# A language-model block on one core: a new order for the first four batches, and the last batch's expert results gathered from blocks kept in order

## The reference

```python
h = tok_ref(x, quantum_params, post_w, post_b)            # gather angles, circuit, 6 -> 192
h = h + attn_ref(layernorm(h), W_qkv, b_qkv)              # one head of 192, softmax(q k / sqrt(192)) v
gate = layernorm(h) @ Wg                                  # 8 scores; the top 2, softmax over them
h = h + sum_k share_k * (gelu(layernorm(h) @ W1[e_k] + b1[e_k]) @ W2[e_k] + b2[e_k])
```

## Time and profile before

| what | us |
|---|---|
| median of 3 runs (lowest, highest) | 286.31 (284.52, 288.8) |
| the profiled execution | 288.43 |
| its span, first to last instruction | 286.7 |
| PE busy (share of the span) | 209.2 (73%) |
| DVE busy | 171.9 (60%) |
| ACT busy | 120.8 (42%) |
| POOL busy | 200.2 (70%) |

### The profile page before, as it was taken

One profiled execution on the slowest core, in us unless ns is written; L12 is line 12 of the kernel. 1 busy time (PEld: TensorE's weight loads), 2 busy tenths in 40 slices (PEclk: granted clock), 3 DMA queues, 4 the chain that ended last, 5 costly groups with the idle time before them and its releaser, 6 DMA issues.

```text
span 286.7 us, 5700 instructions
## 1 busy us (share of the span) xinstructions
PE 209.2 (73%) x1559; PEld 149.3 (52%) x1559; DVE 171.9 (60%) x651; ACT 120.8 (42%) x293; POOL 200.2 (70%) x273
## 2 busy tenths in 40 slices
PE   0760599278877699698688899999999999992000
PEld 0550454123444244445446797787899998982000
DVE  5754899978797995856755586233477003532223
ACT  1001213454454332656446364655566676661000
POOL 5777787707992657477676777777777777777750
PEclk9999999755596755779656799999999999999555
DMA  7911001189900000000012211133333229985763
GB/s 152 297 24 14 4 3 13 13 322 363 322 8 1 9 13 14 9 14 14 13 39 52 56 37 27 43 99 90 102 89 92 76 75 328 351 247 165 237 223 117
DMA packets 26074, 29.85 MB, mean 104 GB/s; under 512 B 15162, under 2 KB 19889, under 8 KB 25851
## 3 DMA queue, kind: packets, MB, share of 16 engines
q1 hardware_dynamic: 19564, 21.54, 24.7%
q0 software_dynamic: 6480, 7.94, 9.2%
HBM read 14.13 MB, written 16.02 MB: 105 GB/s over the span
## 4 chain that ended last, share of the span: by engine, by line
PE 49%; DVE 23%; POOL 9%; issue 7%; ACT 5%; DMA 4%; DVEq 1%; POOLq 0%; ACTq 0%; SPq 0%
PE bank_b L2132 22%; PE bank_b L1886 6%; PE bank_a L2120 5%; POOL circuit L562 5%; PE bank_a L1893 4%; POOL shares_out L767 4%; PE bank_c L1905 3%; DVE nmax L1194 3%; ACT prob L1602 2%; DMA shares_out<-circuit,up 2%; PE bank_d L1844 2%; ACT keys_t L1580 1%; DVE circuit L881 1%; DVE form_s L1165 1%; DVE form_p L1161 1%
## 5 line engine op out<-in xcount | busy, mean ns | idle before, releaser
L767 POOL DMA_INDIRECT shares_out<-circuit,up x71 | 73.7, 1038 | 21.6 <-issue 16.8
L733 POOL DMA_INDIRECT routed<-rows,slot x64 | 62.5, 976 | 31.0 <-issue 16.5
L2132 PE MATMUL bank_b<-wide,up 128*128 x426 | 79.1, 336 | 1.7 <-issue 1.4
L2132 PEld LDWEIGHTS bank_b<-wide,up 128*128 128x128 f32 x426 | 68.9, 192 | 7.2 <-issue 5.5
L1765 ACT ACTIVATE circuit<-bank_b,up 128x192 f32<-128x192 f32 x71 | 29.9, 422 | 29.5 <-PE bank_b L2132 28.0
L562 POOL DMA_INDIRECT circuit<-angles,ids x32 | 31.7, 991 | 11.0 <-issue 9.1
L1753 ACT ACTIVATE up<-bank_a 128x384 f32<-128x384 f32 x71 | 34.3, 486 | 9.0 <-PE bank_a L2120 8.4
L1893 PE MATMUL bank_a<-keys_t,wt 32*128 32x512 f32 x64 | 27.4, 944 | 3.3 <-ACT keys_t L1580 1.9
L1886 PE MATMUL bank_b<-queries_t,keys_t 32*128 32x512 f32 x64 | 25.1, 866 | 4.9 <-ACT keys_t L1580 2.5
L1194 DVE TENSOR_REDUCE nmax<-bank_a 128x2 f32<-128x1024 f32 x16 | 19.5, 1219 | 9.3 <-PE bank_a L1893 9.3
L1602 ACT ACTIVATE prob<-bank_b 128x1024 f32<-128x1024 f32 x16 | 16.4, 1023 | 18.8 <-PE bank_b L1886 18.8
(11 more groups left out here) (438 smaller groups left out, 379.1 us busy)
## 6 DMA issues: line engine op xcount, KB each, us to landing
routed<-pad_rows SPq DMA_DIRECT2D x8, 528.0 KB, 5.3
out<-hres SPq DMA_DIRECT2D x7, 384.0 KB, 5.7
wide<-down_w SPq DMA_DIRECT2D x1, 2304.0 KB, 11.9
prob<-shares_out SPq DMA_DIRECT2D x3, 768.0 KB
up<-up_w SPq DMA_DIRECT2D x1, 1536.0 KB
angle_stages<-shares_out SPq DMA_DIRECT2D x2, 768.0 KB, 6.8
form_p<-shares_out SPq DMA_DIRECT2D x2, 768.0 KB, 6.8
up<-routed SPq DMA_DIRECT2D x71, 16.0 KB, 1.8
```

The costliest lines, as they stand in the source:

```text
L733: pool.indirect_dma_start(out=routed, out_offset=bass.IndirectOffsetOnAxis(slot[:, b, k, j:j + 1], 0), in_=rows[:, b, k, j, :], in_offset=None
L767: pool.indirect_dma_start(out=shares_out, out_offset=bass.IndirectOffsetOnAxis(xb[:, m, DEST:DEST + 1].bitcast(I32), 0), in_=y[:, m % RESU ...
L2132: mm = pe.matmul(bank_b[:, m % 2, 0:D], hid[:, m % STEP, c * P:(c + 1) * P], wide_flat[:, bass.ds(first + c * D, D)], start=(c == 0), stop ...
```

## The change

Four parts. (1) A new order of PE, DVE and ACT for batches 0 to 3 and the start of 4 and 5; new helpers issue all four row groups of one batch (`whole_scores`, `whole_transposed`) or a half of each of two batches (`crossed_scores`), with PSUM banks chosen by `score_bank` and `transposed_bank`. (2) POOL scatters only blocks 0 to 62 to `shares_out`. SP also writes blocks 24 to 70 as they are to `kept` in DRAM, in ten groups of four and three parts. (3) DVE works out for each token of the last batch the row of `kept` in which each of its two results lies (`last_places`, after step 9's `expert_up`). (4) POOL gathers them with eight indirect DMAs straight into SBUF; DVE adds from there.

```diff
+    SCATTERED = 2 * TILES * (BATCHES - 1) + E - 1
+    KEPT_FIRST = EARLY
+    KEPT_RING = RESULTS // STEP
+    PLACED_AT = LOADED_STEPS + 6
...
+        KEPT_GROUPS = [(m, m + STEP) for m in range(KEPT_FIRST, last_until(0) - STEP + 1, STEP)]
+        KEPT_TAIL = [(last_until(x - 1) if x else KEPT_GROUPS[-1][1], last_until(x)) for x in range(len(LAST_PARTS))]
...
+        def score_bank(b, h):
+            if (b, h) == (1, 0):
+                return bank_a[:, 2:4, :]
+            return bank_b[:, :, :] if (b, h) in ((0, 1), (1, 1), (4, 1)) else bank_a[:, 0:2, :]
...
         @block.sync
...
+            def keep(first, last, done):
+                n = first % RESULTS
+                sp.wait_ge(y_done, last)
+                sp.dma_start(kept_view[:, first - KEPT_FIRST:last - KEPT_FIRST, :], y[:, n:n + last - first, :]
+                             ).then_inc(done, 16)
...
+            keep_behind = {EARLY + 30: 0, EARLY + 37: 1, EARLY + 43: 2}
             for m in range(EARLY, BLOCKS):
                 load_block(m)
+                if m in keep_behind:
+                    keep_group(keep_behind[m])
+            for g in range(len(keep_behind), 6):
+                keep_group(g)
...
+            keep_group(8)
+            store(2)
+            keep_group(9)
+            all_added(sp, blocks_until(4 * TILES), blocks_until(5 * TILES))
+            load_sums(5)
+            keep_last(0)
+            keep_last(1)
+            keep_last(2)
+            store(3)
+            all_added(sp, blocks_until(5 * TILES), blocks_until(6 * TILES))
+            load_sums(6)
+            for b in range(BATCHES - 1 - SUMS, BATCHES - 1):
                 store(b)
...
         @block.gpsimd
...
-            for m in range(BLOCKS):
+            for m in range(SCATTERED):
                 pool.wait_ge(y_done, m + 1)
...
+            pool.wait_ge(place_done, 1)
+            pool.wait_ge(exp_done, 2 * BATCHES)
+            for r in range(KEPT_RING):
+                pool.wait_ge(kept_out[r], 16 * len(range(r, len(KEPT_GROUPS), KEPT_RING)))
+            for x in range(len(LAST_PARTS)):
+                pool.wait_ge(kept_last[x], 16)
+                hold(pool)
+                for j in range(LAST_UPTO[x] - LAST_PARTS[x], LAST_UPTO[x]):
+                    for k in range(2):
+                        pool.indirect_dma_start(
+                            out=late_sums[:, k, j * D:(j + 1) * D], out_offset=None,
+                            in_=kept[0:(last_until(x) - KEPT_FIRST) * P, :],
+                            in_offset=bass.IndirectOffsetOnAxis(place[:, k, j:j + 1], 0)
+                            ).then_inc(final_in if (j, k) == (TILES - 1, 1) else last_in[x], 16)
...
         @block.vector
...
+            reduce_angles(2)
             row_max(0, 0)
-            reduce_angles(2)
             row_max(0, 1)
...
+            chain_link(1, 1)
             row_max(1, 0)
-            chain_link(1, 1)
             row_max(1, 1)
             spread_max(1)
+            context(0)
             chain_link(1, 2)
+            variance2(0)
+            row_max(2, 1)
+            route(0)
             row_max(2, 0)
-            chain_link(1, 3)
-            chain_link(1, 4)
-            context(0)
-            row_max(2, 1)
             spread_max(2)
-            chain_ends(1)
-            row_max(3, 0)
-            variance2(0)
-            route(0)
-            context(1)
             normed(0)
-            row_max(3, 1)
-            spread_max(3)
             slots(0)
             shares(0)
+            context(1)
+            chain_link(1, 3)
+            variance2(1)
+            row_max(3, 1)
+            route(1)
+            row_max(3, 0)
+            spread_max(3)
+            chain_link(1, 4)
+            normed(1)
+            chain_ends(1)
             chain_close(1)
+            context(2)
             both_ends(1)
             variance1(1)
-            context(2)
-            variance2(1)
+            variance2(2)
             form(1, 0, E)
             features(2)
-            route(1)
-            features(3)
-            normed(1)
             slots(1)
             shares(1)
-            variance2(2)
+            features(3)
+            context(3)
+            route(2)
+            normed(2)
+            variance2(3)
             row_max(4, 0)
-            route(2)
-            context(3)
             row_max(4, 1)
             spread_max(4)
-            row_max(5, 0)
-            normed(2)
-            variance2(3)
             slots(2)
             shares(2)
+            route(3)
+            row_max(5, 0)
+            normed(3)
+            slots(3)
             row_max(5, 1)
             spread_max(5)
-            route(3)
-            normed(3)
-            slots(3)
+            shares(3)
             row_max(6, 0)
-            shares(3)
...
                 expert_up(s)
+                if s == PLACED_AT:
+                    last_places()
...
         @block.scalar
...
                 if m >= RESULTS:
                     act.wait_ge(added[m % RESULTS], 16 * (m // RESULTS))
+                if m >= KEPT_FIRST + RESULTS:
+                    g = (m - RESULTS - KEPT_FIRST) // STEP
+                    act.wait_ge(kept_out[g % KEPT_RING], 16 * (g // KEPT_RING + 1))
...
         @block.tensor
...
+                if b == 1:
+                    pe.wait_ge(rank_read, 1)
...
+            factor(0)
+            keys(0)
+            whole_scores(0)
+            factor(1)
+            keys(1)
+            queries(0)
+            whole_transposed(0)
+            whole_scores(1)
+            context(0)
+            factor(2)
+            keys(2)
+            merged(0)
+            a_transpose(0)
+            queries(1)
+            gram(0)
+            crossed_scores(1, 0)
+            factor(3)
+            keys(3)
+            crossed_scores(1, 1)
+            ranks(0)
+
             context(1)
-            both_scores(2, 3, 0)
             merged(1)
             a_transpose(1)
-            both_scores(2, BATCHES, 1)
+            queries(2)
             gram(1)
-            ranks(0)
-
+            crossed_scores(2, 0)
+            crossed_scores(2, 1)
+
+            context(2)
+            merged(2)
             queries(3)
-            context(2)
-            both_scores(3, BATCHES, 0)
-            merged(2)
             a_transpose(2)
-            both_scores(3, BATCHES, 1)
+            whole_transposed(3)
             gram(2)
+            ranks(1)
+            context(3)
+            merged(3)
             factor(4)
             keys(4)
-            ranks(1)
-            both_scores(BATCHES, 4, 1)
-            context(3)
-            merged(3)
-            both_scores(BATCHES, 4, 0)
+            a_transpose(3)
+            whole_scores(4)
             factor(5)
             keys(5)
-            a_transpose(3)
+            gram(3)
             ranks(2)
             both_scores(BATCHES, 5, 1)
-            gram(3)
             a2_transpose(0)
...
+            ranks(3)
             both_scores(4, 6, 1)
-            ranks(3)
             a2_transpose(1)
```

More of the change, by code:

```diff
@@ L375, in build @@
         sums_in = [sem(f"sums_in{n}") for n in range(SUMS)]
+        kept_out = [sem(f"kept_out{g}") for g in range(KEPT_RING)]
+        kept_last = [sem(f"kept_last{x}") for x in range(len(LAST_PARTS))]
+        place_done = sem("place_done")
         last_in = [sem(f"last_in{x}") for x in range(len(LAST_PARTS))]
+        final_in = sem("final_in")
         sum_done = sem("sum_done")
@@ L521, in _ @@
                 load_sums(b)
[L522 to L528, removed]
-                store(b)
[L530 to L536, removed]
+            keep_group(6)
+            store(0)
+            load_sums(3)
+            keep_group(7)
+            store(1)
+            all_added(sp, landed, blocks_until(4 * TILES))
+            load_sums(4)
+            keep_group(8)
[10 more added lines that the diff above has]
+            for b in range(BATCHES - 1 - SUMS, BATCHES - 1):
+                store(b)
             for x in range(len(LAST_PARTS)):
@@ L1523, in add_last @@
                 b = BATCHES - 1
[L1524 removed]
                 own = last_tiles(x)
[L1526 to L1527 removed]
+                final = x == len(LAST_PARTS) - 1
+                dve.wait_ge(last_in[x], 16 * (2 * LAST_PARTS[x] - final))
+                step(dve.tensor_tensor(hres[:, b, own], hres[:, b, own], late_sums[:, 0, own], ALU.add))
                 join()
[L1529 removed]
+                if final:
+                    dve.wait_ge(final_in, 16)
@@ new lines, in both_scores, with scores, transposed_scores @@
+                    if 0 <= bs < BATCHES:
+                        scores(bs, 1 - h, n)
+            def scores(b, h, n):
+                j = 2 * h + n
+                r = slice(j * F, (j + 1) * F)
+                mm = pe.matmul(score_bank(b, h)[:, n, :], wt[r, b % 2, :], keys_t[r, b % 3, :], start=True, stop=True)
+                if n == 1:
+                    mm.then_inc(s_done, 1)
```

(36 more changed lines are left out.)

167 lines of the change are left out of this document (93 added, 74 removed).

## The result

The changed kernel takes 302.72 us (median of 4 runs, 301.26 to 303.19), the kernel before 287.1 beside it: ratio 1.0538, 95% interval 1.0491 to 1.0585, slower. Executions over 1.5% above the fastest of their kernel are left out of the ratios, not out of the medians. The profiled execution took 302.79 (span 301.1), 14.4 more than that of before.

What follows compares the result with a forecast made beforehand. The prediction took batch 5's gates plus one unbroken POOL stream plus a tail as the bound: 288.43 + 13.7 (D) - 4.5 (tail) = 297.6, less 2.1 to the median, 295.5 us; own range 291 to 300, whole range 278 to 303.

Steps and rivals of the forecast that it cites:

- The bound: The end is when batch 5's gates are ready, plus one unbroken POOL stream, plus a tail of round trips.
- D: Delay of batch 5's gates by the new order: +7.5 (upper clock) to +19.9 us (lower), taken as 13.7.
- first row scatter near 89: POOL starts scattering batch 0 when its tensor work ends, near 89.0 instead of 94.14 us.
- `features(2)` 104.55 to 109.5: Start of batch 2's features, 100.44 us before: +4.1 at the upper clock level, +9.1 at the lower.
- `queries(4)` 117.1 to 126.5: Batch 4's queries, at 115.01 us before: +2.1 at the upper clock level, +11.5 at the lower.
- The clock: TensorE's clock over batches 1 to 4: the middle between upper and lower level was taken, giving D = 13.7.
- The place: On DVE, batch 5's maximum behind shares(2) and route(3): queries(4) to both_scores(4, 5, 0) about 6 us, 1.74 before.
- The tail, -4.5: Last batch: gathers replace the last scatters' landing and read-back; gain 4.7 us, less 0.2 for extra DMA traffic.
- The third rival: The tail gains 0 because late stores or a slow gather end last: 300 us, chance 0.06.
- some 10 us of cover: Last write of kept rows, waiting for block 70 (260.54), lands that long before POOL's last gathers want it near 274.
- The 2.1 us: Taken off the sum because the profiled execution lay that far over the median of the runs shown (286.31).
- The second rival: POOL's stream closes up from the early batches on if queries(4) comes under 107.5; 276.8 us at 102.5; chance 0.18.

Runs made afterwards that it cites:

- e1_order: The changed kernel with parts 2 to 4 undone: new order, old tail; 299.49 us, ratio 1.0431 to the kernel before.
- after_again: The changed kernel run once more without any edit, beside the next group of runs; 300.09 us, ratio 1.0446 to the kernel before.
- e4_max5: The changed kernel with row_max(5, 0) put back right behind spread_max(4) on DVE; 297.75 us, ratio 1.0353 to the kernel before.
- v1_earlier: The changed kernel with row maxima of batches 4 to 6 and slots(1) moved ahead, plus three more DVE moves; ratio 0.9999 to the kernel before.
- e2_tail: The kernel before with parts 2 to 4 alone: old order, new tail; 287.08 us, ratio 1.0002 to the kernel before.

## Why the prediction was right, and where it was not

Slower, by an order that brings batch 5's gates later: that was right, step by step. The total, 295.5, was 7.2 us low: outside the forecast's own range (291 to 300) and 0.3 us inside the whole one (to 303). That the whole range held the result is in part luck; the second four executions of the same kernel lie at 300.1.

- The bound: right. From batch 5's first scatter to the end it was 135.45 us before and 135.42 after; 135.0, 135.1 and 135.1 in `e1_order`, `after_again` and `e4_max5`. In the other profiles with as many indirect DMAs it was 133.9 to 135.8, in `v1_earlier` 137.1.
- D: predicted 13.7, measured 14.43, then 11.8 in the second profile and 11.7 with the order alone. The steps against the earlier trace rows: first row scatter near 89, it was 86.60 (POOL's tensor work ended at 86.1, not near 89); `variance1(1)` 99.0 to 102.45, it was 99.53; `features(2)` 104.55 to 109.5, it was 106.37; `queries(4)` 117.1 to 126.5, it was 121.70; `both_scores(4, 5, 0)` +6.3 to +16.1, it was +11.1; end of `row_max(6, 0)` +7.5 to +19.9, it was 140.64, +14.4. All but the first lie in the bounds, the last three near the middle.
- The clock: the middle was right for another reason than given, so that D came out close is luck. The granted clock was 0.55, near its lower level, and the layout at that level had said 19.9. Its steps were too long: +9.1 to `features(2)` where 5.9 were measured, 2.4 more to `queries(4)` where it was 0.8, 4.6 where it was 4.4, 3.75 where it was 3.3.
- The place: `row_max(5, 0)` behind `shares(2)` and `route(3)` was priced at about 6 less 1.74 = 4.3 us; the first trace shows 4.4, and putting it back moved batch 5 by 4.3 against that trace, but by 1.7 against `after_again`, and the time by 2.3.
- The tail, -4.5: this term failed, and it is most of the miss. Its parts held: the gather's issue 1.05, the last one's landing 3.6 where 3.3 was taken, last addition 4.05 behind POOL's last issue against a layout of 3.7. But the sum took the last store for the end, and POOL's close stands 8.5 us behind POOL's last instruction, in the trace of before already, 0.55 us ahead of the end of the last store. That row was not read. So at most 0.55 was to be had, and 0 came (`e2_tail`). The third rival, no tail, 300, had the effect, by another cause, and too small a chance.
- Kept rows: "some 10 us of cover" was wrong. TensorE and ACT finished block 70 at 279.15, 18.6 us later than the earlier trace rows, 4 more than D, and with the tail alone 2.6 later (263.16) although batch 5 came 2.3 earlier. The first gather waited 1.22 us. With the order alone block 70 is 11.6 later, as much as D, so the new tail is what makes TensorE late. In the tail alone it falls behind between 215 and 250 us, where the share of the DMA engines is 0.74 against 0.53 before; whether that is the cause was not tried.
- The sum redone: 288.43 + 14.43 + 0 = 302.86; the profiled execution took 302.79. The 2.1 us taken off for the median of before did not come off here: 4.5, 2.1 and 0.7 of D make up the miss of 7.2 to 0.1.
- As to what would show it: POOL's idle time ahead of batch 1 was 12.63 (over 8 was said), ahead of batch 4 4.61, where more was said; the gaps ahead of batches 2 and 3 (6.25, 5.04) lay between.
- The second rival's turning point (`queries(4)` under 107.5) was not reached (121.70): POOL's stream did not close up, its idle time ahead of the row scatters grew.

## What to carry to other kernels

In an order written by hand for several batches, look for a maximum, copy or rank that the next batch's matmul needs and that is queued behind an older batch's bookkeeping: in the profile it is a long-running engine that waits for a short instruction. Move that one ahead; here such moves took 8 us out of 300. Before shortening a tail, read each engine's close at the end of the program, not just the last store: this program ended with the latest of them. Where one queue sets the end, a change that puts as many instructions on it as it takes off gives nothing, however much shorter the data's way becomes.

## What the runs showed of the hardware

- POOL's drain at the end of the program ends 8.4 to 8.8 us behind POOL's last instruction in thirteen profiles (9.7 in one), whether that is an indirect DMA or a product; a drain in the middle of the program ended 2.7 us behind.
- Indirect gathers of 768-byte rows: 0.95 to 1.4 us of POOL, 0.3 between, 3.9 to 4.7 us from issue to landing beside other traffic (medians of the seven profiles with eight of them), where a 384 KB store took 5.7 to 7.1 (medians).
- The same kernel's profile showed a clock of 0.93 in one execution and 0.50 in another over the same 8 us (110 to 118), with 2.7 us between their times at batch 5's first scatter.
